# A Mamba scan on one core: diagonals of C on the matrix engine in place of weighed states, and normalised rows written by ScalarE

## What is computed

```python
def step(h, inp):                       # h: (batch, 512 channels, 16 states)
    d_t, u_t, B_t, C_t = inp
    dA = jnp.exp(d_t[..., None] * A)
    h = dA * h + (d_t * u_t)[..., None] * B_t[:, None, :]
    y = jnp.einsum('bdn,bn->bd', h, C_t)
    return (h, y)
...
y = (ys + us * D[None, None, :]) * _silu(zs)
out = jnp.einsum('md,lbd->lbm', out_proj_w, y)
...
x = _layernorm(x + mamba(x))            # x1 below
x = _layernorm(x + cross_attention(x, ctx))
x = _layernorm(x + ffn(x))
```

## Time and profile before

| what | us |
|---|---|
| three runs, median (lowest to highest) | 492.42 (491.68 to 494.4) |
| the profiled execution | 493.22 |
| its span, first to last instruction | 491.4 |
| busy: PE, DVE, ACT, POOL | 415.2, 390.7, 296.8, 215.7 |
| the scan, five steps from gate to gate, 91.47 to 202.57 | 111.10 |
| from there to the load of the rope tables, 232.91 | 30.34 |
| attention and feed-forward, 237.50 to the end | 253.9 |

### The profile page before, as it was taken

The page is one execution under the profiler, slowest core; times in us unless marked ns, Lnnn a source line. Parts: engine busy times, 40 slices in busy tenths (PEclk is TensorE's granted clock), DMA queues, the critical chain, the costliest instruction groups (busy, mean ns, idle before and its releaser), DMA issues.

```text
span 491.4 us, 11537 instructions
## 1 busy us (share of the span) xinstructions
PE 415.2 (84%) x4148; PEld 341.4 (69%) x4148; DVE 390.7 (80%) x744; ACT 296.8 (60%) x699; POOL 215.7 (44%) x157
## 2 busy tenths in 40 slices
PE   4978973587886977969999999999999999999853
PEld 1435532556675866958888888988888888888642
DVE  1876869999999999998466477879878787987675
ACT  3635997899999999995034445453554545354530
POOL 2400003997979797987333332331424233132101
PEclk9989995598798998799999999999999999999955
DMA  8970373116210241101400000000000000000000
GB/s 280 379 302 3 127 226 107 53 43 144 84 53 18 72 158 45 36 29 36 143 1 4 1 13 1 12 13 12 11 0 21 0 11 11 11 11 0 23 1 22
DMA packets 18659, 30.94 MB, mean 63 GB/s; under 512 B 2113, under 2 KB 11713, under 8 KB 17921
## 3 DMA queue, kind: packets, MB, share of 16 engines
q1 hardware_dynamic: 18624, 30.49, 18.8%
HBM read 24.16 MB, written 6.32 MB: 62 GB/s over the span
## 4 chain that ended last, share of the span: by engine, by line
PE 55%; DVE 18%; ACT 14%; issue 9%; DMA 2%; POOL 1%; DVEq 0%; SPq 0%; POOLq 0%; ACTq 0%
PE ps L452 46%; ACT hc L940 5%; PE ps L574 4%; DVE reg_b L1362 4%; PE ps L688 3%; ACT ps L932 3%; DVE ps L1355 2%; DVE ps L1352 2%; DVE reg_b L1296 2%; DVE reg_b L1249 1%; DMA xw<-x_fm 1%; ACT reg_b L912 1%; DMA reg_a<-rope_q 1%; ACT reg_b L1036 1%; POOL reg_b L1155 1%
## 5 line engine op out<-in xcount | busy, mean ns | idle before, releaser
L1155 POOL TENSOR_TENSOR reg_b<-reg_c,reg_a 128x1024 f32<-128x1024 f32 x56 | 130.5, 2373 | 60.4 <-DVE reg_c L1301 60.3
L1178 POOL TENSOR_TENSOR reg_b<-reg_b 128x768 f32<-128x768 f32 x32 | 57.9, 1810 | 117.0 <-DVE reg_b L1434 117.0
L452 PE MATMUL ps<-x1T,Mw 128*128 (+1 forms) x768 | 93.1, 278 | 1.1 <-DVE reg_b L1434 1.1
L452 PEld LDWEIGHTS ps<-x1T,Mw 128*128 128x128 f32 x768 | 88.3, 192 | 3.9 <-DVE reg_b L1434 1.8
L574 PE MATMUL ps<-ident,hc 128*128 128x128 f32 x456 | 72.7, 309 | 16.6 <-ACT hc L940 15.3
L574 PEld LDWEIGHTS ps<-ident,hc 128*128 128x128 f32 x456 | 59.3, 159 | 27.1 <-ACT hc L940 23.9
L940 ACT ACTIVATE hc<-reg_b,bc 128x512 f32<-128x512 f32 x96 | 68.8, 717 | 6.9 <-DVE reg_b L1362 3.4
L1362 DVE SCALAR_TENSOR_TENSOR reg_b<-reg_c,bc,ps 128x512 f32<-128x512 f32 x96 | 70.8, 742 | 0.0
L932 ACT ACTIVATE ps<-reg_b 128x512 f32<-128x512 f32 x112 | 65.8, 592 | 6.9 <-POOL reg_b L1155 6.1
L1355 DVE TENSOR_TENSOR ps<-ps,reg_b 128x512 f32<-128x512 f32 x80 | 55.3, 697 | 0.1
L1036 ACT ACTIVATE reg_b<-ps,small 128x128 f32<-128x128 f32 x128 | 45.3, 373 | 12.8 <-DVE small L1439 12.8
(11 more groups left out here) (150 smaller groups left out, 677.3 us busy)
## 6 DMA issues: line engine op xcount, KB each, us to landing
reg_a<-a_dram SPq DMA_DIRECT2D x4, 1024.0 KB, 7.8
Mw<-w_o SPq DMA_DIRECT2D x1, 2048.0 KB, 15.9
ud_dram<-reg_b SPq DMA_DIRECT2D x4, 512.0 KB, 4.0
zs_dram<-x1T SPq DMA_DIRECT2D x4, 512.0 KB, 3.7
ud_t<-ud_dram SPq DMA_DIRECT2D x8, 256.0 KB, 2.8
zs_t<-zs_dram SPq DMA_DIRECT2D x8, 256.0 KB, 2.7
xw<-x_fm SPq DMA_DIRECT2D x2, 512.0 KB, 5.7
mring<-w_q SPq DMA_DIRECT2D x4, 256.0 KB, 3.8
```

The lines of the kernel that those rows point to most:

```text
L452: return pe.matmul(o, l, r, start=start, stop=stop)
L1155: pool.tensor_tensor(dA[:, g % RING], delta_r[:, bass.ds(t, 1), :].to_broadcast([P, SA, DI]), Abc[:, g * SA:(g + 1) * SA, :], ALU.mult).th ...
L1178: pool.tensor_tensor(rq[:, g % 2].rearrange("p a c n -> p (a c n)"), pc[:, g % 2].rearrange("p a c n -> p (a c n)"), psn[:, g % 2].rearran ...
```

## The change

- ACT no longer multiplies the state by C. For each state it writes a 128x128 diagonal matrix, the identity times the column of C (`diagonal`), into its own sixteenth of `hc`, right behind the exponential of the same state. It waits until PE has read the diagonal that stood there, of the step before.
- PE no longer turns weighed states: it multiplies the four 128x128 blocks of the state itself, as weights, by the diagonal (`weighed_sum`), an ordinary fp32 product that turns and weighs at once. It waits for the diagonal and for DVE's `state_add`.
- DVE's `state_add` now waits until PE has read the old state (`y_s`) where it waited for ACT's `weigh`.
- In steps 1 to 7 ACT writes the rows x1 of tiles 0 to 6 (`norm1`, as rstd times x plus a shift), at the end of its step, where DVE wrote them in the middle of its own. For the shift POOL computes minus mean times rstd, one instruction more a step, and `rs1` counts two a step. Tile 7's rows stay with DVE.
- PE turns x1 behind state 13 instead of 11, in the last step behind the whole sum; ACT copies the turned x1 (`take_x1`) behind state 1 of the next step instead of at the end of the same one.
- The last step's products on DVE wait for a little more of PE's sum, since all of `hc` now holds diagonals.

```diff
-                    state_sum((n + 1) % WRING, hc_s, NST * (t - 1) + n + 2, n == NST - 1)
+                    weighed_sum(t, n)
...
-                    elif n == 11:
+                    elif n == 13:
                         turn_x1(t - 1)
...
-                elif n == 13:
-                    turn_x1(T - 2)
+            turn_x1(T - 2)
...
+            def weighed_sum(t, n, Y=ps[:, 4, :]):
+
+                pe.wait_ge(hc_s, NST * (t - 1) + n + 2)
+                pe.wait_ge(h_s, NST * (t - 1) + n + 1)
+                for c in range(CI):
+                    last = pe.matmul(Y[:, c * P:(c + 1) * P], H[:, n, c * P:(c + 1) * P], diag_c[:, n, :],
+                                     start=False, stop=n == NST - 1, skip_group_check=True)
+                last.then_inc(y_s, 1)
...
-            def weigh(t, n):
-
-                act.wait_ge(h_s, NST * (t - 1) + n + 1)
-                need(act, y_s, NST * (t - 1) + n + 2 - WRING)
+            def diagonal(t, n):
+
+                if t == 1 and n == 0:
+                    act.wait_ge(y_s, 1)
+                if t > 1:
+                    act.wait_ge(y_s, summed(t - 1, n))
                 s = NST + n
-                act.activation(hc[:, (n + 1) % WRING, :], H[:, n, :], ACT.Copy,
-                               scale=bc[:, t, s:s + 1]).then_inc(hc_s, 1)
+                act.activation(diag_c[:, n, :], ident[:, :], ACT.Copy, scale=bc[:, t, s:s + 1]).then_inc(hc_s, 1)
...
+            def norm1(t):
+
+                act.wait_ge(rs1, 2 * t + 2)
+                need(act, x1_out, 16 * t)
+                need(act, x1Tm, t)
+                act.activation(x1[:, :], ps[:, 6, 0:DM], ACT.Identity, scale=rstd, bias=shifted).then_inc(x1_s, 1)
...
-                    if n >= BEHIND and t < T - 1:
-                        weigh(t, n - BEHIND)
-                    elif n < BEHIND and carried:
-                        weigh(t - 1, NST + n - BEHIND)
+                    if t < T - 1:
+                        diagonal(t, n)
...
-                take_x1(t - 1)
+                    if n == 1 and carried:
+                        take_x1(t - 2)
+                norm1(t - 1)
...
                 rstd_of(veps, rstd, ln1, 3 * t, rs1)
+                pool.wait_ge(rs1, 2 * t - 1)
+                pool.sem_inc(pool_passed, 1)
+                pool.tensor_scalar(shifted, aggr[:, 0:1], rstd, -1.0, ALU.mult, ALU.mult).then_inc(rs1, 1)
...
-                    dve.wait_ge(hc_s, NST * (t - 2) + n + 2)
+                    dve.wait_ge(y_s, summed(t - 1, n))
...
-                    elif n == 11:
-                        norm1(t - 1)
```

More of the change, by code:

```diff
@@ L130, in decoder_layer @@
         deq_sq = small[:, 19:20]
+        shifted = small[:, 7:8]
         stats2, aggr2 = small[:, 48:54], small[:, 54:56]
@@ L168, in decoder_layer @@
         wup_raw, wdn_raw = kvT[:, :, :].rearrange("p t n -> p (t n)"), hc[:, 2:4, :].rearrange("p s d -> p (s d)")
+        diag_c = hc[:, :, :].rearrange("p s (i n) -> p (s i) n", n=P)
         ctx_s = yT[:, :, :].rearrange("p c n -> p (c n)").rearrange("p (t d) -> p t d", t=T)
@@ L311, in work_of, with summed @@
             return last_work if isinstance(t, int) and t == T - 1 else loop_work
+        def summed(t, n):
+            return NST * (t - 1) + n + 2
         def last_slot(n):
@@ L1024, in _ @@
                     take_side(per_step * (T - 2) + ACT_SIDE.index(n))
+            take_x1(T - 2)
             take_x1(T - 1)
@@ L1386, in norm1 @@
             def norm1(t):
-                dve.wait_ge(rs1, t + 1)
+                dve.wait_ge(rs1, 2 * t + 1)
                 need(dve, x1_out, 16 * t)
@@ L1395, in last_state @@
                 dve.wait_ge(da_s, NST * (T - 2) + n + 1)
-                dve.wait_ge(hc_s, NST * (T - 3) + n + 2)
-                dve.wait_ge(y_s, NST * (T - 2) + 1 + n + int(n > FRESH) - WRING + 1)
+                dve.wait_ge(y_s, NST * (T - 2) + 1 + max(n + int(n > FRESH) - WRING + 1, min(0, n - 2)))
                 dve.scalar_tensor_tensor(hc[:, last_slot(n), :], ps[:, n % RING, :], step_b(T - 1, NST + n), H[:, n, :],
@@ L1407, in last_step @@
                         norm1_stats(T - 2)
-                    elif n == 13:
-                        norm1(T - 2)
             def scan_step(t):
```

## The result

The changed kernel takes 509.53 us (median of 4 runs, 508.77 to 514.63), the kernel before beside it 492.68 (4 runs): a ratio of 1.0364, with a 95% interval of 1.0314 to 1.0414. The forecast was 506, with 498 to 512 as its range.

The account below looks back on a forecast made before the run. DVE bounds the scan before; after, a loop through PE, ACT and DVE. Loop 7.8 + step 1's clock 2.7 + two falls 3.4 + scan's end 0 = 13.9 us on 492.4: 506, range 498 to 512.

Parts of the forecast that it names:

- the rival with four falls: PE's clock falls at every long wait for the gate: 7.8 + 2.7 + 6.8 = 17.3 us, 509.7; chance 0.20.
- The product's price: On PE, weighing a state by products against its diagonal costs 0.90 us instead of 0.43 for four transposes.
- The rivals with a cheaper or a dearer product: Cheaper: at most 0.69 us a state, DVE stays bound, 490.7, chance 0.13; dearer: four transposes a product, 577, chance 0.01.
- The loop: Gate-to-gate chain: PE 15.5 plus side jobs, ACT 0.9, DVE 4.5; steps 22.7 to 24.4 us, +7.8 in all.
- The loops' sum: Five scan steps: +7.8 us at full clock, +2.7 for step 1's lower clock, +3.4 for two falls; 13.9 in all.
- the 0.4 us a step that I kept for the range: ACT's diagonal behind exponential 2 stands in the loop: up to 0.4 us a step, 2 us in all, outside the sum.
- The falls: PE's clock drops to 0.50 after long waits at gates: two taken, 1.7 us each, +3.4; chance of one to three 0.45.
- The clock holds: Rival: PE's clock stays up once it is up, 7.8 + 2.7 = 10.5 us, so 502.9; chance 0.20.
- What costs nothing: ACT's diagonal writes, DVE's saved 0.45 us a step, `state_add`'s new wait and SP's later x1 store: no change in time.
- The scan's end: From the fifth window's end to the rope tables: 30.1 us by POOL, 29.9 by PE, 30.34 before; taken as 0.

Follow-up runs that it names:

- the run with the late copy: Changed kernel with ACT's copy of the turned x1 behind state 7 instead of state 1: 496.73 us, ratio 1.0067 to the kernel before.
- The run with half the products: Changed kernel, but PE multiplies only two of each state's four blocks by its diagonal, the other 256 channels left out: 492.46 us, ratio 1.0006.
- the run with the late copy and mended diagonals: Changed kernel with ACT's x1 copy behind state 7 and step 1's first four diagonals behind its fourth exponential: 493.99 us, ratio 1.0042.
- diagonals alone: Kernel before with only PE's products against diagonals; x1 rows on DVE, turn and copy at their old places: 499.75 us, ratio 1.0151.

## Why the prediction was right

The median, 509.53, lies 3.5 us above the forecast and beside the 509.7 of the rival with four falls. The trace of the profiled execution decides between them: it has two falls, and what lies above the forecast is spread over the loops, the scan's end and the rope tables.

- **The product's price** was right: 0.89 us a state, taken as 0.90 from the row of four products of the same form. The rivals with a cheaper or a dearer product fall with it.
- **The loop** was right in its links and its lengths: PE 20.15, ACT 0.91, DVE 4.55 us against 20.0, 0.9 and 4.5. The run with the late copy shows that it was the cause: it moves one copy and nothing else, and 14.0 of 15.3 us go. The run with half the products shows the other end of it: with PE early, DVE is the bound and the loss is gone.
- **The loops' sum was 1.4 us too low** (13.9 against 15.3). Steps 1 and 2 have most of it, 0.6 and 0.55. In step 1 a side job P costs 1.01 from start to start (99.75 to 100.76 in PE's order of time) where I took 0.92 for a row less its tail, three times; an N costs 1.05 instead of 0.96. In step 2 DVE waits a second time, 0.25 us (137.19), since ACT writes a diagonal and copies a side job N between the exponentials 2 and 3: part of the 0.4 us a step that I kept for the range.
- **The falls** were right in number and nearly in price (1.4 and 1.6, taken as 1.7). The number is in part luck: two was chosen between none and four, and which waits would be followed by a fall was left open. PE's waits ahead of the five gates were 2.70, 2.97, 2.82, 1.98 and 2.82 us, as forecast near 2.7 and 1.9; the clock fell at the second and the third.

```profile
117.20 0.66 PE L580 MATMUL ps<-ident,ud_t 128*128 128x128 f32 x4 [2.70 <-DVE yT L1396]
...
140.45 1.11 PE L580 MATMUL ps<-ident,ud_t 128*128 128x128 f32 x4 [2.97 <-DVE yT L1396]
...
216.50 0.66 PE L580 MATMUL ps<-ident,ud_t 128*128 128x128 f32 x4 [2.82 <-DVE yT L1396]
```

- **"The clock holds"** fell as a rival. The Trainium skill, page "TensorE: Matmul & The Clock Gate", section "Part 4: PE-mode transpose", has transposes not count as PE activity, by which products in their place would keep the clock up. The trace of the changed kernel, with its two falls, speaks against that use of it, and so does the run with half the products: PE adds up the states by products alone there, and the mean granted clock of its steps is 0.88 to 0.91, with a fall at each gate, where PE waits 3.7 to 4.6 us. Still the clock of the steps rose, from 0.77 to 0.92 before to 0.90 to 1.00. Before, stretches at 0.50 also began inside steps, at 127.7, 148.3 and 192.6 us, among waits of PE for ACT's weighed states, which the prediction's account of the falls leaves out:

```profile
127.59 1.01 PE L574 MATMUL ps<-ident,hc 128*128 128x128 f32 x4 [0.83 <-ACT hc L940]
...
PE ps L574 <- ACT hc L940: 15.3, 28, 1.2
```

  The changed kernel has none of these waits, and both its falls lie within 1.3 us of a gate. Whether the kind of instruction has a part in it stays open: no run gives transposes and products the same waits.
- **"What costs nothing" had one miss:** `diagonal` in step 1 waits for step 0's sum, 1.03 us between the first two skip sums. The prediction weighed `state_add`'s new wait and found it free; of `diagonal`'s wait for PE it said nothing, and in step 1 one of the places in `hc` is still in use. The first gate came earlier all the same, since the stage ahead ended 2.4 us sooner in this execution (first skip sum at 81.19 instead of 83.61); in the other kernels it lies between 82.1 and 85.7, whatever they change.
- **The scan's end** was taken as 0 and measured 0.38. Up to POOL's deviation it took 8.40 us (forecast 8.45), and the shift was priced from a row that didn't fit:

```profile
224.90 0.55 POOL L1183 TENSOR_TENSOR small<-small 128x1 f32<-128x1 f32 x1 [4.44 <-DVE small L1406]
225.66 0.27 POOL L1194 TENSOR_SCALAR small<-small 128x1 f32<-128x1 f32 x1 [0.21 <-POOL small L1183]
226.24 18.66 POOL L1178 TENSOR_TENSOR reg_b<-reg_c,reg_a 128x1024 f32<-128x1024 f32 x8 [0.31 <-issue]
...
247.19 1.50 SPq L429 DMA_DIRECT2D reg_a<-rope_q  x1
```

  The instruction takes 0.27 us, half of the 0.55 that I gave it, but 0.21 ahead of it and 0.31 behind it are idle: from the deviation to the multiplications 1.34 us, 0.58 before. This pair of dependent instructions cost its gaps as well.

The sum on the profiled execution, 13.9 forecast, 15.5 measured (508.77 - 493.22), is thus right in its main term and short by 1.4 in the loops, 0.4 at the end and 1.0 in the rope tables' transfer, less the 1.4 of the earlier first gate. The median of the runs lies another 0.8 above the profiled execution; the traces don't show why.

## What to carry to other kernels

When an operation gets dearer on an engine that seems to have room, look for the loop that it closes: here ACT, whose exponentials stand behind the copy in its stream, had to wait for PE's late turn before it could go on feeding DVE, and DVE's gate let PE start. Where the consumer of a late result stood in another engine's stream was worth as much as the result's price; six states further on, the same copy waited for nothing. Padding that filled an engine's waits turned into delay once the waits were gone, so mends should be tried one by one.

## What the runs showed of the hardware that was not expected

- Waits of 2.82 us were followed by a fall of the clock once and not once (ahead of 166.06 and of 216.50), 2.70 by none and 2.97 by one; the second fall began at 167.3, 1.2 us after PE had started again. In the run with the late copy and mended diagonals the clock fell behind a wait of only 1.29 us (ahead of 138.16), and with the late copy alone it held behind 1.30 (ahead of 140.60). The length of the last wait alone doesn't tell a fall.
- SP's issue of the first rope table took 1.50 us in the changed kernel and 0.97 to 1.21 in three of its variants (late copy, diagonals alone, late copy with mended diagonals), 0.37 in all others. In those four DVE had the tables 5.0 to 5.6 us after the issue began, in the others 4.2 to 4.6. Why wasn't tried and stays open.
- ACT writes 128x256 values with a scale and a bias in 0.56 us, and copies as many in 0.38; both read PSUM.
